# Gate and up of batches 2 and 3 by seven products of quarters in place of eight

## The chip, the cores and the metric

The kernel runs on one core of one Trainium2 chip. The metric is the device time of one execution in microseconds (us). Engines: TensorE (PE; its weight loads are PEld), VectorE (DVE), ScalarE (ACT), GpSimd (POOL) and SyncE (SP), which issues DMAs.

## The reference

One decoder layer, float32, 4 batches of 512 tokens of width 512:

```
x = layernorm(x + attention(x; Wqkv, bqkv, Wo, bo))        # 16 heads of 32
x = layernorm(x + wkv(w, u, k=x, v=ctx))                   # recurrence along the tokens
g = x @ Wg.T;  u = x @ Wu.T                                # 512 -> 2048, Wg = (gate_w - 128) * gate_scale
x = layernorm(x + (silu(g) * u) @ Wd.T)                    # 2048 -> 512
```

## The kernel before

Every engine's instruction stream is written out from one list of pieces, `tt.order`, that `timetable()` makes: tables of slot numbers at the head of the file (QK_AT, WKV_AT, YT_AT, X2_AT and others) say at which slot a piece is added, and each engine's block walks the list and issues what is its own. So each engine does its pieces strictly in the list's order, and waits on semaphores for the others.

Slots 0 to 255 are the attention of the 16 groups of heads (scores, exponentials, transposes, products with V), with the projections of later batches between them. From slot 256 on, four batches follow in turn: 16 tiles `it` of 128 gate and up features (`gu`, `gate_up`, L838), then four products with the down weights (`y`, L860 and L862; the last of all is cut in quarters, `y_quarters`, L849 and L851). Between them stand the recurrence of later batches (`wkv`: `ek` on ACT, `scan_q` and `scan_p` with the two scans L1181 and L1189, and four reciprocals L1195 in `divide`), and the transposes `yt` and `x2t`.

A token value is held as a high and a low half in float16 (x2h, x2l), transposed, so that each weight tile is multiplied with both. One tile `it` of one batch is, for gate and again for up, 4 tiles of the inner dimension by 2 halves: 16 matmuls of 128x128 weights by 512 tokens. Each half tile of a product fills one of the 8 PSUM banks, and `unit` gives a product the bank that is emptied first. For gate ACT takes silu out of PSUM (`th`, L1014); DVE multiplies by the up product in PSUM (`hf`, L1222); ACT makes the high half of the result (`hh`, L1024) and POOL the low one (`hl`, L1433). Nothing on PE waits for these but the down products and the reuse of banks.

Of the kernel before, what the change touches and what calls it, by code (L numbers as in the profile page):

```python
# [19 lines left out]
EPS = 1e-5  # L20
EOFF = {0: 0, 1: 128, 2: 384, 3: 768}
# [23 lines left out]

EARLY = 4


W_SPLIT = (6, 7, 8, 11)
V0_AT = (0, 8)  # L50
QK_AT = {2: (8, 17), 3: (10, 27), 4: (38, 48), 5: (57, 63), 6: (67, 75), 7: (79, 85), 8: (105, 112), 9: (124, 131),
         10: (136, 144), 11: (146, 151), 12: (166, 175), 13: (173, 195), 14: (195, 199), 15: (212, 228)}
V_AT = {1: (50, 57, 59, 82), 2: (117, 125, 132, 140), 3: (181, 195, 199, 205)}
WO_AT = {0: (86, 96, 100, 103), 1: (152, 154, 155, 168), 2: (203, 212, 216, 224)}
EARLY_AT = (246, 256)

FIN_AT = {0: (3, 0, 10), 1: (3, 2, 13), 2: (2, 0, 11), 3: (2, 0, 12), 4: (2, 1, 4), 5: (1, 0, 3), 6: (3, 1, 10),
          7: (4, 2, 10), 8: (3, 0, 14), 9: (4, 2, 5), 10: (1, 0, 7), 11: (4, 1, 7), 12: (3, 3, 6), 13: (3, 12, 15),
          14: (4, 2, 13)}

LAST_AT = (5, 5, 6)
WAIT = {'high': 1, 'low': 1, 'vtake': 1, 'r1': 2, 'norm': 4, 'exp': 4, 'eb': 0, 't1': 0, 't3': 0, 'oh': 2, 'ol': 2,
        'ek': 1, 'scan_q': 3, 'scan_p': 6, 'divide': 8, 'r2': 2, 'x2h': 1, 'x2l': 3, 'expand': 0}
WAIT_IN = {'r1': 6, 'norm': 2, 'ek': 1, 'scan_q': 1, 'scan_p': 1, 'divide': 2, 'r2': 0, 'x2h': 2, 'x2l': 2}
PIECE_AT = {'load_second': 41, 'small': 101, 'split_wo': 46, 'load_ds': 229}
WU_AT = (41, 71, 77, 116)
WU_ZERO = (83, 88, 137, 144)
WG_AT = (207, 207, 214, 215)
WG_ZERO = (224, 235, 241, 244)
# [8 lines left out]
YT_AT = {0: (156, 164, 174, 183), 1: (269, 270, 270, 270), 2: (283, 283, 286, 287), 3: (302, 303, 303, 308)}  # L78
X2_AT = {0: (225, 228, 230, 232), 1: (272, 272, 272, 273), 2: (290, 291, 291, 292), 3: (314, 314, 314, 314)}
WO_IN = (10, 11, 11, 14)  # L80
ZERO_IN = (8, 9, 11, 12, 12, 12, 12, 14, 14, 14, 14, 14, 14, 14, 14, 14)

KEYS = (0, 0, 0, 0)

TURN = ((4, 6, 5), (3, 4, 6), (3, 6, 5), (3, 4, 4))

OH_POOL = (1, 1, 0, 1, 0, 1, 1, 1, 0, 0, 0, 1, 0, 1, 1, 0)
XH_POOL = (0, 1, 1, 1)

COPIES = (5, 2, 0, 4, 1, 1, 0, 0, 0, 0, 0, 2, 2, 0, 0, 1)  # L90
# [53 lines left out]
def on_dve(H, item):  # L144
# [15 lines left out]
    "x2t": lambda b, c: ("x2l", b, c),  # L160
# [9 lines left out]
def timetable():  # L170
# [376 lines left out]
def build(nc, ctx, xT, x, ctxT, wqkv, bqk, bv, wo, bo, wcol, ucol, gateT, gsc, upT, usc, downT, dsc,  # L547
# [130 lines left out]

    def split_from(p):
# [15 lines left out]
    def stacked(n, kind, r):  # L695
# [3 lines left out]
                SCR[n, "qk".index(kind)][part].rearrange("(h p) t -> p h t", p=32))  # L699

# [3 lines left out]
    def _(e):  # L704
# [137 lines left out]

        def y_cut(q):
# [27 lines left out]
        for name, *a in tt.order:  # L871
# [41 lines left out]
    def _(e):  # L913
# [90 lines left out]

        def th(b, it):
# [600 lines left out]
```

## Time and profile before

| | us |
|---|---|
| median of 3 runs | 727.84 |
| lowest, highest | 725.76, 728.02 |
| profiled execution | 728.07 |
| its span, first to last instruction | 726.0 |
| PE busy | 707.3 |
| DVE, ACT, POOL busy | 510.8, 409.0, 303.2 |

The span is what the trace shows; 2.1 us lie around it. Matmuls overlap in the trace: one of 512 columns is listed with 0.38 us though the next starts 0.216 us later. So PE's busy time says when it has work, and not how fast it goes: that is read from the distance between starts.

### The profile page before, as it was taken

The page shows a single profiled execution, that of the slowest core. Times are in us where ns is not written, and L with a number is a line of the kernel's source. Part 1 is how long each engine was busy: PE and PEld are TensorE (multiplying, and loading weights), DVE is VectorE, ACT ScalarE, POOL GpSimd, SP SyncE. Part 2 cuts the span into 40 slices and gives each one's busy share as a digit, 9 for nine tenths or more (in the row PEclk, how much of TensorE's full clock was granted, in tenths as well). Part 3 has the DMA queues.
Part 4 walks back from the last instruction along what each step waited for, and adds up shares of the span by engine and source line. Part 5 has one row for each costly group of instructions (what it writes and reads, how often), then busy time and mean ns, then how long its engine had stood idle before and what let it go on. Part 6 is the DMA issues. An engine that isn't in the chain of part 4 may idle for free.

```text
span 726.0 us, 11976 instructions
## 1 busy us (share of the span) xinstructions
PE 707.3 (97%) x4274; PEld 391.4 (54%) x4274; DVE 510.8 (70%) x1191; ACT 409.0 (56%) x980; POOL 303.2 (42%) x338
## 2 busy tenths in 40 slices
PE   8898999999999999998999999999999999999997
PEld 3466665666665666666554445445544444544445
DVE  3588766799899889899826889866787734532224
ACT  5478877769886787679755662154612532133310
POOL 2016421464766314541356834474645733023310
PEclk9999999999999999999999999999999999999999
DMA  7728739344233234643044010000001000100001
GB/s 230 227 87 212 241 73 242 86 123 117 66 92 115 51 104 130 143 76 88 3 63 112 1 59 15 30 16 1 0 16 44 0 1 1 43 16 1 0 15 44
DMA packets 45530, 54.16 MB, mean 75 GB/s; under 512 B 4896, under 2 KB 34848, under 8 KB 45472
## 3 DMA queue, kind: packets, MB, share of 16 engines
q1 hardware_dynamic: 41632, 46.59, 21.9%
q0 software_dynamic: 3264, 6.29, 5.1%
q10 hardware_dynamic: 576, 0.52, 0.3%
q8 instruction: 34, 0.56, 0.3%
q14 instruction: 24, 0.20, 0.1%
HBM read 47.10 MB, written 12.58 MB: 82 GB/s over the span
## 4 chain that ended last, share of the span: by engine, by line
PE 87%; DVE 4%; ACT 3%; DMA 2%; issue 2%; SPq 1%; POOL 1%; ACTq 0%; POOLq 0%; DVEq 0%
PE psb L838 29%; PE psb L726 10%; PE psb L764 8%; PE psb L862 7%; PE psb L860 7%; PE psb L742 6%; PE psb L809 5%; PE psb L777 5%; PE psb L753 4%; PE psb L825 2%; PE psb L797 2%; PE psb L788 2%; DMA ks<-parts 1%; ACT ee L949 1%; DVE st L1143 1%
## 5 line engine op out<-in xcount | busy, mean ns | idle before, releaser
L1098 DVE CUSTOM_DVE_ANT_0 ee<-psb,mask,clip 128x512 f32<-128x512 f32 (+3 forms) x256 | 130.6, 535 | 20.7 <-PE psb L753 20.1
L949 ACT ACTIVATE ee<-ee,nm 128x512 f32<-128x512 f32 (+3 forms) x256 | 142.0, 559 | 1.5 <-DVE nm L1098 1.5
L1433 POOL TENSOR_TENSOR hl<-hf,hh 128x512 f16<-128x512 f32 x64 | 74.2, 1160 | 103.6 <-ACT hh L1024 103.6
L1024 ACT ACTIVATE hh<-hf 128x512 bf16<-128x512 f32 x64 | 40.3, 630 | 119.6 <-DVE hf L1222 115.1
L960 ACT ACTIVATE ee<-psb 128x256 f32<-128x256 f32 (+1 forms) x156 | 81.5, 531 | 42.7 <-PE psb L764 36.3
L764 PE MATMUL psb<-ident,ee 128*128 128x128 f32 x640 | 98.9, 274 | 3.3 <-DVE ee L1112 1.5
L1222 DVE SCALAR_TENSOR_TENSOR hf<-th,c,psb 128x512 f32<-128x512 f32 x60 | 43.7, 729 | 79.8 <-PE psb L838 63.2
L838 PE MATMUL psb<-x2h,wg 128*128 128x512 f16 x256 | 97.0, 379 | 0.0
L838 PE MATMUL psb<-x2h,wu 128*128 128x512 f16 x256 | 97.0, 379 | 0.0
L838 PE MATMUL psb<-x2l,wg 128*128 128x512 f16 x256 | 97.0, 379 | 0.0
L838 PE MATMUL psb<-x2l,wu 128*128 128x512 f16 x256 | 97.0, 379 | 0.0
L860 PE MATMUL psb<-wd,hh 128*128 128x512 f16 x240 | 91.0, 379 | 0.0
L862 PE MATMUL psb<-wd,hl 128*128 128x512 f16 x240 | 91.0, 379 | 0.0
L764 PEld LDWEIGHTS psb<-ident,ee 128*128 128x128 f32 x640 | 75.2, 141 | 24.1 <-ACT ee L960 3.0
L753 PE MATMUL psb<-ks,qs 128*128 128x512 f16 (+3 forms) x256 | 73.9, 300 | 4.0 <-DMA ks<-parts 2.5
L726 PE MATMUL psb<-xh,wqk 128*128 128x512 f16 x256 | 65.9, 384 | 2.1 <-ACT xh L921 1.1
L1195 DVE RECIPROCAL ek<-ek 128x128 f32<-128x128 f32 x64 | 58.0, 930 | 5.4 <-POOL ek L1401 5.4
L1385 POOL TENSOR_TENSOR rs<-ve,half 128x1 f32<-128x1 f32 (+1 forms) x24 | 17.3, 719 | 97.1 <-DVE ve L1163 96.9
L1014 ACT ACTIVATE th<-psb,g 128x512 f32<-128x512 f32 x60 | 40.8, 680 | 28.9 <-PE psb L838 28.7
L949 ACT ACTIVATION_READ_ACCUMULATOR ee<-ee,nm 128x1 f32 x256 | 50.7, 198 | 0.0
L838 PEld LDWEIGHTS psb<-x2l,wu 128*128 128x128 f16 x256 | 25.1, 98 | 29.9
L838 PEld LDWEIGHTS psb<-x2h,wu 128*128 128x128 f16 x256 | 25.1, 98 | 29.9
(130 smaller groups left out, 1215.7 us busy)
## 6 DMA issues: line engine op xcount, KB each, us to landing
qs<-parts SPq DMA_DIRECT2D x64, 128.0 KB, 2.9
ks<-parts SPq DMA_DIRECT2D x60, 128.0 KB, 3.4
parts<-qhl SPq DMA_DIRECT2D x16, 256.0 KB, 2.1
parts<-khl SPq DMA_DIRECT2D x16, 256.0 KB, 2.3
x<-in_x SPq DMA_DIRECT2D x4, 1024.0 KB, 6.9
ct<-in_ctxT SPq DMA_DIRECT2D x4, 1024.0 KB, 5.3
out<-x SPq DMA_DIRECT2D x16, 256.0 KB, 2.0
xt<-in_xT SPq DMA_DIRECT2D x14, 256.0 KB, 4.2
```

The costliest lines, as they stand in the source:

```text
L726: mm = e.matmul(PSB[:, bk, :], wt[:, k, c0:c0 + P], xt[:, k, :], start=(p == 0 and k == 0), stop=(p == 2 and k == T - 1))
L753: e.matmul(PSB[:, bank["score", H, i], 0:w], QS[:, sl, h, i * P:(i + 1) * P], KS[:, sl, h, 0:w], start=True, stop=True).then_inc(sem("scor ...
L764: mm = e.transpose(PSB[:, bk, o:o + P], E[H % 3][:, EOFF[i] + j * P:EOFF[i] + (j + 1) * P], IDENT[:])
L838: mm = e.matmul(PSB[:, bk, :], wt[:, k, it * P:(it + 1) * P], xt[:, s, k, :], start=(k == 0 and xt is x2h), stop=(k == T - 1 and xt is x2l))
L860: e.matmul(PSB[:, bk, :], HS[it][0][:, t * P:(t + 1) * P], wd[:, it, :], start=(it == 0), stop=False)
L862: mm = e.matmul(PSB[:, bk, :], HS[it][1][:, t * P:(t + 1) * P], wd[:, it, :], start=False, stop=(it == IT - 1))
L949: e.activation(dst, dst, ACT.Exp, bias=NM[:, n % 4, col:col + 1], scale=-1.0, accum_out=DEN[:, n % 4, col:col + 1]).then_inc(sem("exp"), 1)
L960: e.activation(ET[h][:, base:base + width], PSB[:, bank["turn", H, item], 0:width], ACT.Copy).then_inc(sem("et"), 1)
L1098: e.tensor_tensor_reduce(E[H % 3][:, EOFF[i]:EOFF[i] + w], PSB[:, bank["score", H, i], 0:w], MASK[:, S - w:S], -SC, CLIP[:, i:i + 1], ALU. ...
L1195: e.reciprocal(EK2S[c % 2][:, cut], EK2S[c % 2][:, cut]).then_inc(sem("rcp"), 1)
L1222: e.scalar_tensor_tensor(out=half[:], in0=gated[:], scalar=col, in1=PSB[:, bank["up", b, it], :], op0=ALU.mult, op1=ALU.mult).then_inc(sem ...
L1433: e.tensor_tensor(HS[it][1][:], ring(b, it)[1][:], HS[it][0][:], ALU.subtract).then_inc(sem("hl"), 1)
```

## The change

For batches 2 and 3 (`SEVEN`), gate and up are taken together as one product of a 2 by 2 block matrix of weights (gate and up by the two halves of the inner dimension) with a 2 by 2 block matrix of tokens (the same halves by tokens 0 to 255 and 256 to 511), and its four quarters are made from seven products of quarters, not eight. Three of the seven need sums of weight quarters only, made once (`weight_sum`: 8 of 128x2048 float16 values, 4 on DVE, 4 on POOL), three need sums of token quarters (`x_sum`, then high and low halves again), and results are added up in and behind PSUM. A pair `m` is two tiles `it`: seven `product` calls of 8 matmuls of 256 columns. Products 1, 6, 7 and 4 run on in one bank ("sa"), 5 and 3 in another ("sd"), 2 in a third ("sb"). Between them ACT copies the bank's value so far to SBUF (`snap1`, `snap5`, `snap6`) and the next product of the bank waits for that; DVE adds the copies (`c11`, `c12`, `c22`). silu now reads SBUF, two per pair behind `c12`, and the multiplication is cut in halves of 256 tokens (`hfb`, `hfa`). Product 4 of a pair comes in the next pair.

The core of the diff:

```diff
+SEVEN = (2, 3)
-WKV_AT = {(0, 0): 111, (0, 1): 123, (0, 2): 133, (0, 3): 143, (1, 0): 191, (1, 1): 209, (1, 2): 262, (1, 3): 264,
-          (2, 0): 266, (2, 1): 272, (2, 2): 274, (2, 3): 277, (3, 0): 288, (3, 1): 292, (3, 2): 294, (3, 3): 297}
+WKV_AT = {(0, 0): 111, (0, 1): 123, (0, 2): 134, (0, 3): 144, (1, 0): 193, (1, 1): 208, (1, 2): 263, (1, 3): 266,
+          (2, 0): 268, (2, 1): 271, (2, 2): 273, (2, 3): 277, (3, 0): 285, (3, 1): 289, (3, 2): 291, (3, 3): 296}
-REST_AT = (16, 41, 97, 72)
+REST_AT = (0, 36, 92, 13)
...
+    def seven_first(b, m):
+        if m == 0:
+            tt.flush(("xlo", b, 3))
+        for j, name in ((1, "sa"), (5, "sd"), (2, "sb"), (6, None)):
+            if name:
+                tt.unit(name, b, m)
+                tt.unfinished.add((name, b, m))
+            add("p", b, m, j)
+            if j == 2:
+                add("c11", b, m)
+            else:
+                add(f"snap{j}", b, m)
+
+    def seven_second(b, m):
+        for j in (3, 4, 7) if m < PAIRS - 1 else (4, 7, 3):
+            if j == 4:
+                fourth(b, m - 1)
+                continue
+            add("p", b, m, j)
...
+                add("c12", b, m)
+            else:
+                add("c22", b, m)
+        for it in (2 * m, 2 * m + 1):
+            add("silu", b, it)
+        for it in (2 * m - 2, 2 * m - 1) if m else ():
+            add("hh", b, it)
+            add("hl", b, it)
+        for it in (2 * m, 2 * m + 1):
+            add("hfb", b, it)
...
+        def product(b, m, j):
...
+            if j == 6:
+                pe.wait_ge(*by("snap1", b, m))
+            elif j == 7:
+                pe.wait_ge(*by("snap6", b, m))
+            elif j == 4:
+                pe.wait_ge(*by("c22", b, m))
+            elif j == 3:
+                pe.wait_ge(*by("snap5", b, m))
+            for k in (0, 1):
+                for kk in (0, 1):
+                    for low in (0, 1):
+                        mm = e.matmul(PSB[:, bk, k * HALF_S:(k + 1) * HALF_S], weights(j, kk, 2 * m + k),
+                                      moving(b, j, kk, low), start=(unit is not None and k + kk + low == 0),
+                                      stop=(kk + low == 2), skip_group_check=True)
...
+        def silu(b, it):
+            m, k = divmod(it, 2)
+            act.wait_ge(*by("c11", b, m))
+            act.wait_ge(*by("c12", b, m))
+            e.activation(pair(b, m)[:, k, :], pair(b, m)[:, k, :], ACT.Silu, scale=G2[:, it:it + 1]).then_inc(sem("silu"), 1)
```

Nearly all other tables of slots are changed as well (QK_AT, V_AT, TURN and the rest, REST_AT as an example above), so that pieces of the attention stand in another order; COPIES gives DVE 24 of the copies of transposed scores in place of 36, and KEYS gives POOL one multiplication per column tile of batch 0.

Where the last column tile of the recurrence (batch 3) falls in batch 2, DVE's queue held this before (names: hf, the multiplication; ekv, qs_, ps, the recurrence and its scans; ek2, its reciprocals):

```order
L1222 SCALAR_TENSOR_TENSOR hf1<-th1,c2,psb 128x512
L1222 SCALAR_TENSOR_TENSOR hf2<-th2,c2,psb 128x512
L1177 TENSOR_TENSOR ekv<-ek,ct 128x512
L1181 SCALAR_TENSOR_TENSOR qs_<-ew,ek 128x512
L1189 SCALAR_TENSOR_TENSOR ps<-ew,ekv 128x512
L1222 SCALAR_TENSOR_TENSOR hf0<-th0,c2,psb 128x512
L1195 RECIPROCAL ek2_1<-ek2_1 128x128 x2
L1222 SCALAR_TENSOR_TENSOR hf1<-th1,c2,psb 128x512
```

It holds this now (ring01 with 2x256 first `c11`, then `c12`; ct2<-psb `c22`; 128x256 `hfb` or `hfa`):

```order
L1517 TENSOR_TENSOR ring01<-psb,snap1 128x2x256
L1449 TENSOR_TENSOR ekv<-ek,ct 128x512
L1453 SCALAR_TENSOR_TENSOR qs_<-ew,ek 128x512
L1461 SCALAR_TENSOR_TENSOR ps<-ew,ekv 128x512
L1523 TENSOR_TENSOR ring01<-psb,ys 128x2x256
L1529 TENSOR_TENSOR ct2<-psb,ct2 128x512
L877 SCALAR_TENSOR_TENSOR ring01<-ring01,c2,ct2 128x256 x2
L1467 RECIPROCAL ek2_1<-ek2_1 128x128 x2
L1517 TENSOR_TENSOR ring01<-psb,snap1 128x2x256
L1467 RECIPROCAL ek2_1<-ek2_1 128x128 x2
L1523 TENSOR_TENSOR ring01<-psb,ys 128x2x256
L877 SCALAR_TENSOR_TENSOR ring01<-ring01,c2,psb 128x256 x2
```

The recurrence stood behind two multiplications; now it stands between `c11` and `c12` of the first pair, and its reciprocals are on both sides of `c11` of the second.

ACT's queue at the same place before (ek: the two exponentials of the recurrence; th: silu):

```order
L988 ACT_TABLE_LOAD
L988 ACTIVATE ek<-psb,nmu 128x512
L991 ACTIVATE ek2_1<-psb,mu2 128x512
L1014 ACT_TABLE_LOAD
L1014 ACTIVATE th0<-psb,g2 128x512
L1024 ACTIVATE hh2<-hf0 128x512
L1014 ACTIVATE th1<-psb,g2 128x512
L1024 ACTIVATE hh3<-hf1 128x512
```

And now, from the second copy of batch 2's first pair (snap1, ct2 and ys written from psb are the copies, ring01 by g2 silu):

```order
L1253 ACTIVATE ct2<-psb 128x512
L1253 ACTIVATE ys<-psb 128x512
L1196 ACTIVATE ek<-psb,nmu 128x512
L1199 ACTIVATE ek2_1<-psb,mu2 128x512
L1259 ACT_TABLE_LOAD
L1259 ACTIVATE ring01<-ring01,g2 128x512 x2
L1253 ACTIVATE snap1<-psb 128x512
L1253 ACTIVATE ys<-psb 128x512 x2
L1259 ACTIVATE ring01<-ring01,g2 128x512 x2
L1265 ACTIVATE hh0<-ring01 128x512
L1265 ACTIVATE hh1<-ring01 128x512
L1253 ACTIVATE snap1<-psb 128x512
```

The copies of a pair now stand behind silu and `hh` of the pair before, in one queue, and the table load in front of the first silu carries its wait for `c12`.

## Rows read from the trace of the kernel before

**Rows 1.** The page, part 1: busy us (share of the span) xinstructions.
```profile
PE 707.3 (97%) x4274; PEld 391.4 (54%) x4274; DVE 510.8 (70%) x1191; ACT 409.0 (56%) x980; POOL 303.2 (42%) x338
```

**Rows 2.** Windows: us, busy PE, PEld, DVE, ACT, POOL (xinstructions), PEclk, DMA share, GB/s.
```profile
20.00:380.00 360.00, 350.87 (x2482) 218.51 (x2481) 295.75 (x860) 274.33 (x784) 147.95 (x197) 1.00 0.45 116
...
460.00:550.00 90.00, 90.00 (x442) 43.96 (x441) 67.25 (x97) 34.56 (x50) 50.36 (x44) 1.00 0.04 16
550.00:693.00 143.00, 142.99 (x681) 66.94 (x679) 60.96 (x95) 46.63 (x71) 51.54 (x46) 1.00 0.03 10
```

**Rows 3.** The chain that ended last, in order of time: start us, us, what.
```profile
637.50 55.25 PE psb L838 x256
```

**Rows 4.** PE's timeline, the last 128 matmuls (first and last): start us, us, engine.
```profile
713.31 0.22 PE L849 MATMUL psb<-wd,hh 128*128 128x128 f16 x1
...
720.40 0.22 PE L851 MATMUL psb<-wd,hl 128*128 128x128 f16 x1
```

**Rows 5.** PEld's timeline beside them (one of the 128 weight loads).
```profile
713.59 0.10 PEld L849 LDWEIGHTS psb<-wd,hh 128*128 128x128 bf16 x1
```

**Rows 6.** Groups of one shape, ACT: busy us, mean ns, idle before.
```profile
L960 ACT ACTIVATE ee<-psb 128x512 f32<-128x512 f32 x108 | 63.2, 597 | 23.7 <-PE psb L764 23.3
...
L1014 ACT ACTIVATE th<-psb,g 128x512 f32<-128x512 f32 x60 | 40.8, 680 | 28.9 <-PE psb L838 28.7
L1024 ACT ACTIVATE hh<-hf 128x512 bf16<-128x512 f32 x64 | 40.3, 630 | 119.6 <-DVE hf L1222 115.1 <-PE psb L788 4.6
...
L1014 ACT ACT_TABLE_LOAD x9 | 11.5, 1283 | 0.2
```

**Rows 7.** The same, DVE.
```profile
L1222 DVE SCALAR_TENSOR_TENSOR hf<-th,c,psb 128x512 f32<-128x512 f32 x60 | 43.7, 729 | 79.8 <-PE psb L838 63.2 <-ACT th L1014 13.5 <-issue 2.9
...
L1233 DVE TENSOR_TENSOR ys<-psb,bo 128x512 f32<-128x512 f32 x15 | 10.1, 671 | 31.4 <-PE psb L862 31.4
...
L1200 DVE TENSOR_SCALAR wu<-wu 128x2048 f16<-128x2048 f16 x4 | 3.6, 893 | 0.0
...
L1079 DVE SCALAR_TENSOR_TENSOR wv<-ee,wv 128x2048 f16<-128x2048 f32 x1 | 2.3, 2291 | 1.0 <-ACT wv L926 1.0
...
L1253 DVE TENSOR_TENSOR x<-ys,x 128x128 f32<-128x128 f32 x4 | 1.2, 292 | 0.1
```

**Rows 8.** The same, POOL.
```profile
L1433 POOL TENSOR_TENSOR hl<-hf,hh 128x512 f16<-128x512 f32 x64 | 74.2, 1160 | 103.6 <-ACT hh L1024 103.6
L1397 POOL TENSOR_TENSOR ct<-ek,ct 128x512 f32<-128x512 f32 x16 | 32.2, 2011 | 8.8 <-DVE ekv L1177 8.1
```

**Rows 9.** ACT's timeline where its queue is full.
```profile
440.81 0.69 ACT L988 ACTIVATE ek<-psb,nmu 128x512 f32<-128x512 f32 x1 [3.37 <-PE psb L825]
441.40 0.68 ACT L991 ACTIVATE ek<-psb,mu 128x512 f32<-128x512 f32 x1
```

**Rows 10.** DVE's timeline, one column tile of the second stage.
```profile
547.82 0.68 DVE L1177 TENSOR_TENSOR ekv<-ek,ct 128x512 f32<-128x512 f32 x1
...
549.55 2.22 DVE L1189 TENSOR_TENSOR_SCAN ps<-ew,ekv 128x512 f32<-128x512 f32 x1
552.86 2.58 DVE L1195 RECIPROCAL ek<-ek 128x128 f32<-128x128 f32 x3 [1.09 <-POOL ek L1401]
```

**Rows 11.** All engines, where ACT starts behind a gate product.
```profile
663.23 0.38 PE L838 MATMUL psb<-x2h,wu 128*128 128x512 f16 x1
...
663.43 0.69 ACT L1014 ACTIVATE th<-psb,g 128x512 f32<-128x512 f32 x1 [0.26 <-PE psb L838]
```

**Rows 12.** Windows around PE's idle time at 22 us (columns as in rows 2).
```profile
22.00:25.00 3.00, 1.24 (x6) 0.32 (x4) 1.79 (x6) 1.09 (x2) 0.00 (x0) 1.00 0.58 186
25.00:28.80 3.80, 3.73 (x10) 1.38 (x11) 1.35 (x7) 1.80 (x8) 0.00 (x0) 0.55 0.78 208
```

**Rows 13.** PE's timeline there, eight 512-column matmuls.
```profile
25.34 3.52 PE L742 MATMUL psb<-wv,xh 128*128 128x512 f16 x8
```

**Rows 14.** Who PE waited for: us in total, times, longest us.
```profile
PE psb L753 <- DMA ks<-parts: 2.5, 2, 1.5
```

More of the change, by code:

```diff
@@ L20 @@
 EPS = 1e-5
+HALF_S = S // 2
 EOFF = {0: 0, 1: 128, 2: 384, 3: 768}
@@ L44 @@
 OHS = 6
+SEVEN = (2, 3)
+PAIRS = IT // 2
+SIGNAL = {"snap1": "snap", "snap5": "snap", "snap6": "snap", "c11": "summed", "c12": "summed", "c22": "summed"}
+PART_READ = {1: 1, 2: 0, 3: 0, 4: 3, 5: 1, 6: 2, 7: 2}
 EARLY = 4
[L49 to L53, printed above, removed]
@@ L62 @@
[L62 to L69, printed above, removed]
@@ L79 @@
[L79 to L90, printed above, removed]
+LAST_AT = (5, 5, 8)
+WAIT = {'high': 1, 'low': 1, 'vtake': 1, 'r1': 2, 'norm': 6, 'exp': 4, 'eb': 0, 't1': 1, 't3': 0, 'oh': 2, 'ol': 3,
+        'ek': 1, 'scan_q': 2, 'scan_p': 7, 'divide': 8, 'r2': 3, 'x2h': 1, 'x2l': 2, 'expand': 0}
@@ L159 @@
     "yt": lambda b, t: ("r2", b, t),
-    "x2t": lambda b, c: ("x2l", b, c),
+    "x2t": lambda b, c: ("xf" if b in SEVEN else "x2l", b, c),
+    "sa": lambda b, m: ("hfa", b, 2 * m + 1),
+    "sb": lambda b, m: ("c11", b, m),
+    "sd": lambda b, m: ("c12", b, m),
     "gate": lambda b, it: ("aa" if early(b, it) else "th", b, it),
@@ L295, in x2t, with quarters @@
         add("x2t", b, c)
+        if b in SEVEN:
+            late(wait("x2h"), lambda: quarters(b, c))
+            return
         late(wait("x2h"), lambda: add("x2h", b, c))
         late(wait("x2l"), lambda: add("x2l", b, c))
+    def quarters(b, c):
+        add("xf", b, c)
+        if c == T - 1:
+            for k in range(4):
+                add("xhi", b, 0) if k == 0 else None
+                add("xt", b, k)
+                add("xhi", b, k) if k else None
+            for k in range(4):
+                add("xlo", b, k)
     def gu_parts(b, it, pools):
@@ L433, in timetable @@
         piece(max(BO_AT[b], PIECE_AT["split_wo"] + 2), "add_bo", b)
+    for j, slots in WS_AT.items():
+        for kk, slot in enumerate(slots):
+            piece(slot, "ws", j, kk)
     for which, slot in WKV_AT.items():
@@ L1066, in _ @@
                 th(*a)
+            elif name == "xf":
+                x_full(*a)
+            elif name == "xhi":
+                x_part_high(*a)
+            elif name in ("snap1", "snap5", "snap6"):
+                snap(*a, int(name[-1]))
+            elif name == "silu":
+                silu(*a)
+            elif name == "hh" and a[0] in SEVEN:
+                hh_seven(*a)
             elif name == "hh":
@@ L1322, in _ @@
                 hf(*a)
+            elif name == "ws" and not WS_POOL[a[0] - 1]:
+                weight_sum(e, dve, *a)
+            elif name == "xt":
+                x_sum(*a)
+            elif name == "xlo" and not XLO_POOL[a[0]]:
+                x_part_low(e, dve, *a)
+            elif name == "c11":
+                c11(*a)
+            elif name == "c12":
+                c12(*a)
+            elif name == "c22":
+                c22(*a)
+            elif name == "hfa":
+                hf_half(e, dve, *a, True)
+            elif name == "hfb" and not HFB_POOL[a[0]]:
+                hf_half(e, dve, *a, False)
             elif name == "yd":
@@ L1474, in _ @@
                 hl(*a)
+            elif name == "ws" and WS_POOL[a[0] - 1]:
+                weight_sum(e, pool, *a)
+            elif name == "xlo" and XLO_POOL[a[0]]:
+                x_part_low(e, pool, *a)
+            elif name == "hfb" and HFB_POOL[a[0]]:
+                hf_half(e, pool, *a, False)
     @block.sync
```

245 lines of the change are left out of this document (223 added, 22 removed).

## The prediction

> **What bounds the kernel now.** I read the page's busy shares first, then busy time by stage, the chain that ended last, who PE waited for, and at the end single shapes and timelines. PE is busy 707.3 of 726.0 us, DVE 510.8 and the others less [rows 1]. By stage the reader should see that PE is busy 142.99 of the 143 us from 550 to 693, which are batches 2 and 3 almost whole, and all 90 us before them, while DVE, ACT and POOL are there busy 61, 47 and 52 of 143 us [rows 2]. The chain says the same: gate and up of batch 3 are one unbroken piece of 256 matmuls in 55.25 us [rows 3], 215.8 ns each. So in the stage that is changed every 100 ns taken from PE is 100 ns of the span, as long as nothing new makes PE wait. In the attention, 20 to 380 us, PE is without work 9.1 us and DVE is busy 296 of 360 [rows 2].
>
> **What the change takes from PE.** Before, a pair of tiles is 32 matmuls of 512 columns (2 tiles, gate and up, 4 inner tiles, 2 halves): 32 x 0.2158 = 6.91 us. Now it is 7 products of 8 matmuls of 256 columns. No row shows 256 columns in a dense stream, but both sides do: 128 columns start 55.8 ns apart (720.40 - 713.31 over 127 steps [rows 4]), 512 columns 215.8 ns. The line through the two gives 109.1 ns, of which some 2.4 ns don't depend on columns. A pair is then 56 x 0.1091 = 6.11 us, 0.80 less, and for 16 pairs the term is **-12.7 us**. The bounds are 107 ns (half of 512 columns, 14.6 us gained) and 112 ns (twice the 128, 10.1 gained). I take the line, since both its ends are the same kind of float16 stream.
>
> The change doubles the weight loads per column, and a load is listed with 0.10 us [rows 5]. Each of those 128-column matmuls has its own load and they still start 55.8 ns apart, so loads overlap and do not set a distance of 109 ns. The Trainium skill speaks against this: TensorE: Matmul & The Clock Gate, Back-to-back issue gap, says that in a stream of load and matmul pairs the load has its share in the spacing, and gives about 81 ns at 128 columns and 131 at 512. By a line through those (98 ns at 256) the sum would be 16 x (56 x 0.098 - 32 x 0.131) = +20 us, an estimate from that page. The trace has 55.8 and 215.8 at its two points, so I go by the trace.
>
> **What it adds on PE's path: waits.** PE never waited for an elementwise result in gate and up. Now each bank goes on only after ACT has copied it. In a steady pair, product 6 needs snap1, which stands in ACT's queue behind two silu and two `hh` of the pair before, which stand behind `c12`, which stands behind product 3. From product 6 round to the next product 6: two products 1.75 us, handover 0.20 (the gate product ends at 663.23 and ACT starts at 663.43 [rows 11]), `c12` 0.67 like the addition from PSUM [rows 7], then silu, silu, hh, hh, copy. Those take 0.68, 0.63 and 0.60 [rows 6], but in a full queue the next starts 0.09 before the one before it ends (441.40 after 440.81 with 0.69 [rows 9]): 0.59 + 0.59 + 0.54 + 0.54 + 0.60 = 2.86. With 0.1 for two handovers between the others the ring is 5.6 us, against 6.11 that PE needs: no wait, 0.5 to spare. DVE has three additions and four half multiplications (0.44 each, between 292 ns for 128 and 729 for 512 columns [rows 7]), 3.8 of 6.11 us; POOL two `hl` of 1.16 [rows 8].
>
> The exception is the last column tile of the recurrence, which now stands between `c11` and `c12` of the first pair of batch 2. Counting from product 1's start: product 6 ends at 3.49, the transposes at 3.93, ACT's first exponential at 4.82. DVE then has the multiplication and two scans, 3.95 us from 547.82 to 551.77 [rows 10], until 8.8, then `c12` until 9.5. The table load, 1.28 [rows 6], has the wait for `c12` on it: 10.8. Two silu 12.05, snap1 12.6. PE is ready for product 6 at 8.3 and **waits 4.3 us**. In the second pair two of the four reciprocals (0.86 each, three in 2.58 [rows 10]) stand before `c11` and two before `c12`: second `hfb` 12.5, `c11` 15.0, `c12` 17.45, silu, hh and copy 20.3, where PE is ready at 18.7: **1.6 us** more. A residual and a norm before `c11` of the last pair cost 0.3. Sum **+6.2 us**. Bounds: 4 (if DVE starts the scans earlier or the load goes ahead of its wait, 1.3 less) and 10 (no overlap in ACT's queue, where the ring is 5.9, and each handover a little longer).
>
> **What it adds elsewhere, at nothing.** Four weight sums on DVE, of 2048 float16 each, lie between 0.89 and 2.29 us [rows 7], at most 9.2; DVE is idle 22.7 of the 90 us from 460 to 550 [rows 2]. Four on POOL are 4.6 us each by `hl`, up to 8.0 by the slower form [rows 8]; POOL is idle 39.6 of these 90, and a late `hl` holds back only the third multiplication after it, with 8 banks behind that. If that cover were gone, each would cost PE its excess over some 8 us. The sums of tokens (4 copies of 0.60, 4 additions of 0.7, 4 high halves up to 1.1, low halves on POOL 8.1 together) make a chain that ends, by my count, 25.7 us after the down products start, and the products give it 28.1; at POOL's slower rate it would end 4 us late, in each of two batches. These are the bounds, 0 and 8; I take 0. The attention's new order: the 9.1 us of waiting there could shrink or grow. x of batch 0 and of batch 3 are now loaded early, beside the stacks of q and k, for which PE already waited 2.5 us [rows 14]. DVE gives 12 copies of 0.7 to ACT, which has 86 us free. I take 0, between -5 and +5.
>
> **The clock.** In 22 to 25 us PE was busy 1.24 of 3 us at full clock; in the 3.8 us after it the granted clock was 0.55 [rows 12], mostly the 1.2 GHz level, and eight matmuls of 512 columns took 3.36 us to the start of the next work in place of 1.73 [rows 13]. So a wait of 4.3 us may well be followed by such a stretch, which costs 1.6. Here it lands between the two waits, where DVE and not PE sets the end, so I count 0. The Trainium skill (the same page, HAM oscillation) has the rule that idle gaps between bursts put the clock back and the warming is paid again; by it the 1.6 would be paid once per gap, and it would be hidden as above.
>
> **Sum.** 728.07 (the profiled execution, 726.0 of span and 2.07 around it) - 12.7 + 6.2 = 721.6; the median of the runs is 0.2 lower than that execution, and I add 0.5 for handovers not counted: **722**.
>
> **Rivals.**
> 1. *The waits hardly come* (0.20). If the planner's order lets DVE do the scans under product work, or the early stages win a few us, 12.7 stays nearly whole with 1 to 2 of waits: **716**. Against it stand the queues: `c12` cannot pass the scans.
> 2. *The head of batch 2 costs more* (0.14): the token sums are late at POOL's slower rate, or the low clock is not hidden: +3, **725**.
> 3. *The attention loses what the products gain* (0.12): loads beside the stacks and new places cost PE 5 us more. The row for it is the wait for ks; against it, PE is busy 351 of 360 us there. **727.5**, no difference.
> 4. *The ring becomes the bound* (0.07), slower. If silu from SBUF, the strided additions or each handover cost more than their nearest rows, PE waits in all 14 steady pairs. The 6.5 us of gain are gone when the ring is 6.6 us, 1.0 above my count; at 7.1 us it is 14 x 1.0 = 14 more: **735**. Against it: everything in the ring has a row within 10%.
> 5. *Weight loads set the distance* (0.02), slower: with a load of 98 ns before each 56 ns of work it would be 0.154 x 56 = 8.6 us a pair, 27 us more than before: **755**. The 128-column stream speaks against it [rows 4]. It is the skill's rule above.
>
> That the change does not do what it says I rule out: the order of instructions shows 56 matmuls of 256 columns per pair.
>
> **How the numbers follow.** The forecast has 0.45. The range of 8 in 10 leaves out rivals 4 and 5 and the ends of 1: from 715 to 730. A measurement of this kernel can tell 0.3%, some 2.2 us, from no change. Faster: 0.45 + 0.20 + 0.14 = 0.79; the same: rival 3, 0.12; slower: rivals 4 and 5, 0.09.
>
> **What would show it.** In the changed profile: matmuls of 256 columns 109 ns apart; one pair 6.11 us from product 1 to product 1 in batch 3, with PE not waiting; two waits of PE, 4 and 1.6 us, for ACT's copy to snap1 at the head of batch 2, with DVE in the scan and the reciprocals then; the granted clock low behind the first; DVE busier in batches 2 and 3 by some 38 us (16 x 3.8 against 32 x 0.73) and ACT by 29 (16 x 4.42 against 32 x 1.31). It is wrong if PE waits for snap1 in every pair, if the distance is over 112 ns, or if the attention ends more than 5 us earlier or later than 380.

## The result, and the profile after

| | before | after |
|---|---|---|
| median of 4 runs, us | 727.31 | **744.62** |
| lowest, highest | 725.76, 728.02 | 743.99, 746.62 |
| profiled execution (span) | 728.07 (726.0) | 743.99 (742.0) |

The ratio is 1.0246, 95% interval 1.0219 to 1.0272: slower by 17 us, where 722 was forecast and 730 was the end of the range. The page, busy us of each engine:

```profile
PE 703.0 (95%) x4658; PEld 430.2 (58%) x4658; DVE 580.9 (78%) x1259; ACT 444.1 (60%) x1052; POOL 346.7 (47%) x350
```

Against [rows 1], PE has less to do and waits more; DVE is busy 70 us longer and POOL 43, in part because their instructions take longer and not only because there are more of them. The windows, columns as in [rows 2]:

```profile
20.00:380.00 360.00, 348.71 (x2448) 215.70 (x2450) 291.29 (x844) 278.40 (x799) 146.82 (x192) 0.99 0.42 113
...
460.00:550.00 90.00, 87.87 (x424) 42.47 (x422) 78.77 (x100) 36.78 (x52) 69.78 (x50) 0.98 0.03 9
550.00:693.00 143.00, 129.89 (x968) 96.49 (x967) 114.75 (x168) 63.12 (x105) 62.47 (x47) 0.95 0.04 16
```

PE was without work 0 us from 460 to 693 before; now it lacks 2.1 and then 13.1 us, and the granted clock, 1.00 before, is 0.98 and 0.95. DVE is busy 115 of 143 us where it was 61, 54 more and not the 38 of the prediction; POOL's busy time from 460 to 550 rose from 50 to 70 us. Who PE waited for (us in total, times, longest), those that are new or larger; the second and third fall in the attention:

```profile
PE psb L1044 <- ACT snap L1253: 10.1, 3, 8.2
PE psb L932 <- DVE nm L1370: 4.6, 8, 1.4
PE psb L998 <- DMA ct<-in_wo: 2.8, 1, 2.8
PE psb L1044 <- POOL x2l L864: 2.5, 1, 2.5
PE psb L1017 <- DVE x2l L1477: 2.1, 1, 2.1
PE psb L1066 <- DVE x L1422: 1.1, 1, 1.1
PE psb L1044 <- DVE ys L1529: 0.4, 1, 0.4
```

That the products themselves pay as forecast shows in the chain, where PE runs on without a wait (start, us, what), first in batch 2 behind its head, then in batch 3:

```profile
595.42 17.48 PE psb L1044 x160
...
667.64 41.31 PE psb L1044 x376
```

160 matmuls in 17.48 us are 109.3 ns each, 376 in 41.31 are 109.9. Batch 3 takes 49.5 us from its first product at 659.31 to the first down product at 708.79, against 55.25 before [rows 3]: 5.8 gained of 6.35. The loss lies ahead of it: batch 2 begins at 563.5 us, and began at 550.3 before; batch 3 begins at 659.3, and began at 637.3. So 13 us are lost before the first new product, and 9 more in batch 2.

**A norm that takes 4.2 us.** DVE's timeline and POOL's in y of batch 0 (start, us):

```profile
448.41 0.94 DVE L1467 RECIPROCAL ek<-ek 128x128 f32<-128x128 f32 x1
449.27 4.17 DVE L1441 TENSOR_SCALAR x<-x,mv,rs 128x512 f32<-128x512 f32 x1
453.36 0.94 DVE L1467 RECIPROCAL ek<-ek 128x128 f32<-128x128 f32 x1
```

```profile
449.10 4.05 POOL L859 TENSOR_TENSOR s1a<-wu 128x2048 f16<-128x2048 f16 x1
```

The norm of 512 columns has a median of 0.55 us. It takes 4.17 here, and ends 0.3 us after POOL's weight sum, which began just before it, has ended. The same stands at 547.80 (4.16, beside the sum from 547.62 to 551.68). The steps behind it in DVE's queue are late too, for DVE has no gap in its work from there to 471 us: PE waits 1.14 us at 454.90 for a residual and 2.13 at 471.02 for the low half that opens batch 1, and the first matmuls behind that wait are at the low level of the clock (32 of them take 8.6 us, from the start of the first to that of the next work, in place of 6.91).

**The head of batch 2.** All engines, from the token sums to the wait (a few lines of each, in order of time):

```profile
558.51 4.86 POOL L864 TENSOR_TENSOR x2l<-ring,x2h 128x1024 f16<-128x1024 f32 x2
561.43 2.49 DVE L1509 TENSOR_TENSOR snap<-ring 128x512 f32<-128x512 f32 x1
563.34 2.57 POOL L864 TENSOR_TENSOR ct<-ring,ct 128x1024 f16<-128x1024 f32 x1
563.52 0.27 PE L1044 MATMUL psb<-x2h,wg 128*128 128x256 f16 x1 [2.54 <-POOL x2l L864]
563.85 2.34 DVE L1441 TENSOR_SCALAR x<-x,mv,rs 128x512 f32<-128x512 f32 x1
...
573.68 0.68 DVE L1517 TENSOR_TENSOR ring<-psb,snap 128x512 f32<-128x512 f32 x1
574.88 1.22 DVE L1453 TENSOR_TENSOR_SCAN qs_<-ew,ek 128x512 f32<-128x512 f32 x1
576.01 2.22 DVE L1461 TENSOR_TENSOR_SCAN ps<-ew,ekv 128x512 f32<-128x512 f32 x1
578.15 0.66 DVE L1523 TENSOR_TENSOR ring<-psb,ys 128x512 f32<-128x512 f32 x1
578.89 1.28 ACT L1259 ACT_TABLE_LOAD   x1 [8.03 <-DVE ring L1523]
582.06 0.61 PE L1044 MATMUL psb<-ct,s2a 128*128 128x256 f16 x2 [8.18 <-ACT snap L1253]
```

The fourth token sum takes 2.49 us and the norm behind it 2.34, both beside POOL's low halves, and PE waits 2.54 us for those. DVE then works off the last two residuals and norms of batch 1, with two gaps of 0.66 us, and comes to the first `c11` only at 573.68, though PE was through with product 2 at 567.8. From there it goes as the prediction has it: scans, `c12`, table load, copy. PE waits 8.18 us. Behind it 27 matmuls start 0.214 us apart, half the speed, until 587.84: 2.8 us more than at 0.109. Behind the wait of 2.54 it was the same for 3.2 us, 1.6 more.

### The profile page after: what moved, and what is told of

Its sections match the earlier page's. It is cut to its first block, busy times and chain, and to the rows that moved or that the text cites. A ratio compares the mean times of both kernels' runs of the same rounds, so it can differ in the third digit from the quotient of the medians.

```text
span 742.0 us, 13026 instructions
## 1 busy us (share of the span) xinstructions
PE 703.0 (95%) x4658; PEld 430.2 (58%) x4658; DVE 580.9 (78%) x1259; ACT 444.1 (60%) x1052; POOL 346.7 (47%) x350
## 4 chain that ended last, share of the span: by engine, by line
PE 60%; DVE 19%; issue 7%; ACT 5%; DMA 4%; POOL 3%; SPq 1%; ACTq 0%; POOLq 0%; DVEq 0%
PE psb L1044 10%; PE psb L1017 9%; PE psb L905 8%; PE psb L943 7%; PE psb L921 5%; PE psb L988 4%; PE psb L956 4%; DVE x L1441 4%; PE psb L932 4%; PE psb L1068 2%; PE psb L1066 2%; DMA ct<-in_wo 2%; DVE ek L1467 2%; DVE st L1415 2%; DVE ps L1461 2%
## 5 line engine op out<-in xcount | busy, mean ns | idle before, releaser
L1755 POOL TENSOR_TENSOR hl<-ring,hh 128x512 f16<-128x512 f32 x64 | 80.5, 1272 | 94.6 <-ACT hh L1265 55.9
L1168 ACT ACTIVATE ee<-psb 128x512 f32<-128x512 f32 (+1 forms) x168 | 84.4, 526 | 35.4 <-PE psb L943 33.0
L1017 PE MATMUL psb<-x2h,wg 128*128 128x512 f16 x128 | 49.1, 384 | 2.1 <-DVE x2l L1477 2.1
L1017 PE MATMUL psb<-x2l,wg 128*128 128x512 f16 x128 | 49.3, 385 | 0.0
L1017 PE MATMUL psb<-x2h,wu 128*128 128x512 f16 x128 | 48.9, 382 | 0.0
L1017 PE MATMUL psb<-x2l,wu 128*128 128x512 f16 x128 | 48.8, 381 | 0.0
L1441 DVE TENSOR_SCALAR x<-x,mv,rs 128x512 f32<-128x512 f32 x48 | 40.9, 897 | 7.1 <-POOL rs L1707 7.1
L932 PEld LDWEIGHTS psb<-ks,qs 128*128 128x128 f16 x256 | 24.9, 98 | 30.2 <-DVE nm L1370 8.1
L1066 PEld LDWEIGHTS psb<-wd,hh 128*128 128x128 bf16 x240 | 23.5, 98 | 29.0 <-DVE x L1422 1.4
L1068 PEld LDWEIGHTS psb<-wd,hl 128*128 128x128 f16 x240 | 23.5, 98 | 28.5 <-POOL hl L1755 0.9
```

Source lines behind the costliest of these rows:

```text
L932: e.matmul(PSB[:, bank["score", H, i], 0:w], QS[:, sl, h, i * P:(i + 1) * P], KS[:, sl, h, 0:w], start=True, stop=True).then_inc(sem("scor ...
L1017: mm = e.matmul(PSB[:, bk, :], wt[:, k, it * P:(it + 1) * P], xt[:, s, k, :], start=(k == 0 and xt is x2h), stop=(k == T - 1 and xt is x2l))
L1066: e.matmul(PSB[:, bk, :], HS[it][0][:, t * P:(t + 1) * P], wd[:, it, :], start=(it == 0), stop=False)
L1068: mm = e.matmul(PSB[:, bk, :], HS[it][1][:, t * P:(t + 1) * P], wd[:, it, :], start=False, stop=(it == IT - 1))
L1168: e.activation(ET[h][:, base:base + width], PSB[:, bank["turn", H, item], 0:width], ACT.Copy).then_inc(sem("et"), 1)
L1755: e.tensor_tensor(HS[it][1][:], pair(b, it // 2)[:, it % 2, :] if b in SEVEN else ring(b, it)[1], HS[it][0][:], ALU.subtract).then_inc(sem ...
```

## The experiments

Each run was made beside runs of the kernel before on the same chip: e1 to e4 on one (before: 728.2 us), e5 to e8 on a second (726.9), e9 to e12 on a third (726.8). Times are medians; ratios to before with their 95% interval. A difference between two groups is safe to about 1 us: by the ratios e2 less e11 is 3.9 us, by the medians 4.8.

| run | us | ratio |
|---|---|---|
| the change | 744.6 | 1.0246 (1.0219 to 1.0272) |
| e1, weight sums on DVE | 736.1 | 1.0115 (1.0080 to 1.0149) |
| e2, all sums on DVE | 734.4 | 1.0093 (1.0062 to 1.0125) |
| e3, eight products, new order | 735.2 | 1.0119 (1.0082 to 1.0156) |
| e4, scans later | 747.6 | 1.0279 (1.0249 to 1.0310) |
| e5, seven products, old order, sums on DVE | 740.4 | 1.0167 (1.0134 to 1.0199) |
| e6, old order, seven in batch 3 alone | 726.4 | 0.9981 (0.9959 to 1.0004) |
| e7, new order, seven in batch 3 alone | 730.5 | 1.0045 (1.0023 to 1.0066) |
| e8, POOL's weight sums cut in four | 736.9 | 1.0133 (1.0108 to 1.0157) |
| e9, e6 with the sums later | **723.0** | 0.9937 (0.9913 to 0.9960) |
| e10, e2 with the attention's old order | 729.1 | 1.0028 (1.0011 to 1.0044) |
| e11, e2 with the old places of the loads of x | 729.6 | 1.0040 (1.0022 to 1.0059) |
| e12, e2 with short scans | 730.7 | 1.0047 (1.0028 to 1.0067) |

### Do POOL's long instructions hold DVE? (e1, e2, e8)

```diff
-WS_POOL = (1, 0, 0, 1)
+WS_POOL = (0, 0, 0, 0)
```

> All eight weight sums on DVE, none on POOL. Theory L (one long POOL instruction holds up DVE's instructions on SBUF until it ends): DVE's norm steps at 449 and 548 us, 4.17 and 4.16 us in the changed kernel, fall to their usual 0.55, and PE's waits before batch 1's gate (1.1 and 2.1 us) with the slow clock behind them (1.8) go; DVE takes on four sums of 1.2 to 2.2 us. Time 738 to 741, from 744.6. Theory Q (DVE is late because of what stands in its own queue, and the long norm records are only how it waits): the four more sums, some 7 us of DVE work, make it later still, 745 to 749.

e2 has besides:

```diff
-XLO_POOL = (0, 0, 1, 1)
+XLO_POOL = (0, 0, 0, 0)
```

> The weight sums and also the low halves of the token sums on DVE, so POOL does no new work at all. Theory L: the second and third token sums, 2.5 us each beside POOL's low halves, fall to 0.7; the low halves, 2.5 to 4.9 us on POOL, take about 1.1 for 1024 elements on DVE; PE's wait of 2.5 us for them before batch 2 goes, and the first addition c11 of batch 2 comes some 4 us earlier, so the wait for snap1 falls from 8.2 towards the 4.3 that the scans alone cost: 733 to 737. Theory Q: the same DVE queue gets 4 us more per batch: the head waits grow, 746 to 752.

And e8 keeps the sums on POOL:

```diff
-        e.tensor_tensor(WSUM[j][kk], a, c, op).then_inc(sem(f"ws{j}"), 1)
+        for w in range(4 if WS_POOL[j - 1] else 1):
+            cut = slice(w * 512, (w + 1) * 512) if WS_POOL[j - 1] else slice(0, I)
+            ins = e.tensor_tensor(WSUM[j][kk][:, cut], a[:, cut], c[:, cut], op)
+        ins.then_inc(sem(f"ws{j}"), 1)
```

> The changed kernel with each of POOL's four weight sums cut into four instructions of 512 columns; same work, same queue places. Theory L (the two engines hold the way to SBUF for a whole instruction): DVE's norm at 449 and 548 us is held 1.0 to 1.5 us in place of 4.2, and the time is near e1's, 736 to 740. Theory R (they share it, each slowed in proportion): DVE's instructions there are as slow in sum as before, and the time stays 743 to 746.

e1 took 8.5 us off, more than its expectation, and e2 10.2, though both give DVE more to do; so theory Q falls. These two also free POOL's queue, so they don't show by themselves that it is DVE that was held. e8 is the clean test, for it moves no work at all: 7.7 us off. DVE and then POOL in e8 at the place shown above:

```profile
447.78 1.27 DVE L1444 TENSOR_SCALAR x<-x,mv,rs 128x512 f32<-128x512 f32 x1
```

```profile
447.61 4.67 POOL L861 TENSOR_TENSOR s1a<-wu 128x512 f16<-128x512 f16 x4
```

The four pieces take 4.67 us together, against 4.05 for the sum in one, and the norm is held 1.27 us, about one piece. That speaks for a hold by the instruction (L) and against a shared rate (R). In e1 the norm at 452.07 took 0.45. The wait of 2.54 us at the head of batch 2 is gone in e8 as well, though the low halves of the token sums are still on POOL there: it was the weight sum at 547.62, holding the norm, that made them late. The wait for snap1 stays 8.17 us in e8 and 8.2 in e1, so these holds are not its cause. What is left of the waits in e2:

```profile
PE psb L1044 <- ACT snap L1253: 8.0, 2, 7.5
PE psb L1017 <- DVE x2l L1477: 0.9, 1, 0.9
```

The waits before batches 1 and 2 are down to 0.9 and nothing, the token sums to 0.69 each. The wait for snap1, which I expected to fall towards 4.3, fell only to 7.48. That part of the expectation was wrong.

### What makes the wait of 7.5 to 8.2 us? (e4, e12)

```diff
-          (2, 0): 268, (2, 1): 271, (2, 2): 273, (2, 3): 277, (3, 0): 285, (3, 1): 289, (3, 2): 291, (3, 3): 296}
-YT_AT = {... 3: (300, 301, 307, 308)}
+          (2, 0): 268, (2, 1): 271, (2, 2): 273, (2, 3): 277, (3, 0): 285, (3, 1): 289, (3, 2): 291, (3, 3): 299}
+YT_AT = {... 3: (303, 303, 307, 308)}
```

> The last column tile of the recurrence (x1t, exponentials, scans) stands behind the second pair of batch 2 and its reciprocals round the third, in place of between c11 and c12 of the first; its transposes yt of the first two token tiles follow 2 to 3 tiles later. Theory S (the scans behind a late c11 make the wait): the first wait for snap1 falls from 8.2 us to under 3, a wait of 2 to 4 appears behind the second pair instead, where DVE has caught up; in all 3 to 5 us less: 739 to 742. Theory L (DVE is behind by the locked 7 us whatever the order, so the same wait comes at another place): 743 to 746.

747.6, against 744.6 for the change: above both ranges. It is not better; that it is worse isn't shown, since the two intervals overlap. The larger of PE's seven waits for snap1 in e4:

```profile
567.72 0.38 PE L1044 MATMUL psb<-ct,s2a 128*128 128x256 f16 x2 [1.74 <-ACT snap L1253]
577.88 0.39 PE L1044 MATMUL psb<-ct,s2a 128*128 128x256 f16 x2 [4.70 <-ACT snap L1253]
587.50 0.39 PE L1044 MATMUL psb<-ct,s2a 128*128 128x256 f16 x2 [1.24 <-ACT snap L1253]
598.25 0.39 PE L1044 MATMUL psb<-ct,s2a 128*128 128x256 f16 x2 [4.46 <-ACT snap L1253]
```

One wait of 8.2 has become four of 1.2 to 4.7 in the first pairs, and PE's total for snap1 rose from 10.1 to 15.2. Theory S falls: the scans' place alone is not the cause.

```diff
+            w = 8 if (b, c) == (3, 3) else S
-            e.tensor_tensor_scan(QS_[:, 1:S + 1], EW[:, c:c + 1].broadcast_to([P, S]), EK[:], 0.0, ALU.mult,
+            e.tensor_tensor_scan(QS_[:, 1:w + 1], EW[:, c:c + 1].broadcast_to([P, w]), EK[:, 0:w], 0.0, ALU.mult,
...
-            cut = slice(k * P, (k + 1) * P)
+            cut = slice(k * P, k * P + (8 if (b, c) == (3, 3) else P))
```

> e2, where the two scans and four reciprocals of the last column tile of the recurrence do only their first 8 columns (of 512 and of 128), so that the last quarter of v's features is left out. DVE has 3.2 us less between c11 and c12 and 3.0 less round the second pair. Prediction's account of the wait (4.3 us from the scans alone): the wait for snap1 falls from 7.5 to about 4 and the second one stays gone, since c11 itself comes 4 us late out of the y phase: 730 to 732. Rival (ACT's queue, its exponentials and the table load set the wait, not DVE): it stays above 6, 733 to 735.

```profile
PE psb L1044 <- ACT snap L1253: 4.9, 2, 4.4
```

The longest wait went from 7.48 to 4.4 and the time down by 3.6 us. So the scans make 3.1 us of it, and 4.4 us are there without them. About 1 of the 3.1 is again a hold: in e2 the second scan takes 2.23 us beside POOL's product of 2.04 (568.82), and in e12, with the short scans, the same product takes 1.26 (567.02). The 4.4 fit DVE's backlog out of the y phase: in e2, PE is through with the first product 2 at 562.5 and DVE begins the first `c11` at 567.4. No run takes this backlog away, so that part is read from the trace and not tested. ACT's table load (1.28 us) and two silu stand behind `c12` in both runs and are part of what is left; that they set the wait instead of DVE is refuted by the fall of 3.1. In e2 DVE has that backlog without any hold by POOL's sums (columns of windows as in [rows 2]):

```profile
538.00:576.00 38.00, 30.52 (x182) 17.71 (x181) 34.35 (x49) 12.37 (x19) 16.41 (x14) 0.95 0.08 28
```

34.35 of 38 us busy: DVE is close to the bound of this stretch. The corresponding 38 us before (530 to 568) have 31.28, with PE never waiting, since nothing on PE hung on DVE then.

### What does the new order cost? (e3, e10, e11, e5)

```diff
-SEVEN = (2, 3)
+SEVEN = ()
...
-    for j, slots in WS_AT.items():
-        for kk, slot in enumerate(slots):
-            piece(slot, "ws", j, kk)
```

> Eight products in batches 2 and 3 as before and no weight or token sums, but all the changed tables (order of the attention, places of the recurrence). It prices the new order alone. If the order costs what the trace suggests (the attention ends 3.9 us later, and y of batch 0 some 2 more without the sums' part): 731 to 734. If what looked like the order's cost was pressure of the sums on DVE and POOL: 727 to 729. Batches 2 and 3 take 6.91 us per pair again and PE never waits there.

735.2, above the upper branch: the tables alone cost 7 us (6 to 11 by the interval), without one new product or sum. In batches 2 and 3 PE waits for nothing, as expected. The trace has 3.5 us of the loss before the first gate product (355.7 us against 352.2) and 2.6 between there and batch 2. The tables hold more than places: they also give ACT 12 of DVE's copies.

```diff
-REST_AT = (0, 36, 92, 13)
+REST_AT = (16, 41, 97, 72)
```

> e2 with x of batches 0 and 3 loaded at the slots of before (16 and 72 in place of 0 and 13). If these loads delay the load of Wo (PE waited 2.7 us for it) and the stacks: 731 to 733, from 734.4. If Wo's load is late for another reason (its wait for the staged tokens): 734 to 735.

729.6, 4.8 us less than e2 and more than I expected. But I had named the wrong batches; the edit puts back all four. In the changed kernel the last large load ahead of Wo's in SP's queue is that of batch 1, moved from slot 41, where it stood behind Wo's, to 36:

```profile
64.64 0.43 SPq L1853 DMA_DIRECT2D x<-in_x  x1
68.39 0.61 SPq L1859 DMA_DIRECT2D ct<-in_wo  x1
```

In e11 Wo's load is issued at 69.27 us and this one at 76.03. The changed kernel's chain and the timeline of PE behind it; then the same product in the kernel before:

```profile
68.39 14.45 DMA ct<-in_wo
82.97 5.12 PE L998 MATMUL psb<-ct,bv 128*128 128x512 f32 x8 [2.77 <-DMA ct<-in_wo]
```

```profile
80.09 3.60 PE L819 MATMUL psb<-ct,bv 128*128 128x512 f32 x8
```

Wo takes 14.45 us to land, 9.9 before; PE waits 2.77 us, and the eight matmuls behind take 5.12 in place of 3.60, since the clock has fallen (0.84 from 83 to 92 us). In e11 Wo lands after 10.0 us, the wait is gone and they take 3.60 again. That it is this one of the four loads is read from the queue; no run moves it alone.

e10 takes every table of the attention from before (and with it the recurrence's places and others up to slot 255, and the shares of DVE, ACT and POOL), those behind it from the change, and has all sums on DVE.

> Tables of the attention (slots to 255) as before the change, those from slot 256 on as after it; seven products in batches 2 and 3, all sums on DVE. The new order's 7 us from e3 split in two: if they are lost in the attention (the trace shows 3.9 us by its end, PE waiting 4.6 us for the masked scores on DVE and 1.7 to 3 for the load of Wo), this runs at 734.4 - 4 = 729 to 731. If they are lost behind slot 256: 733 to 736.

729.1, only 0.5 us below e11: nearly all that the attention loses lies in the places of these loads. The many short waits for the scores' maxima (nm), 4.6 us in e11 and 2.4 in e10, are worth no more than that. The rest of the 7 us lies behind slot 256.

e5 goes on and takes those as before too (WKV_AT, YT_AT, X2_AT, WAIT_IN, WO_IN, ZERO_IN and LAST_AT).

> Every table of slots as it was before the change; seven products in batches 2 and 3; all weight and token sums on DVE. If the new order costs the 7 us that run e3 showed whatever stands behind it: 734.4 - 7 = 727 to 729. If the new order was what made room for the sums on DVE between 460 and 575 us (there the recurrence's fifteenth column tile stands in the y phase again), the head of batch 2 waits 4 to 6 us longer: 731 to 734.

740.4: wrong in both branches, and the slowest of the runs with all sums on DVE. PE's waits for snap1:

```profile
PE psb L1044 <- ACT snap L1253: 17.6, 4, 15.3
```

With the old places the fifteenth column tile of the recurrence falls into y of batch 1, and one wait, at the head of batch 2, is 15.3 us. DVE begins the first `c11` at 569.39, and in front of the copy ACT now also has a second table load and the exponentials of the last column tile (573.40 to 575.85). So behind slot 256 the new order loses some 2 us by itself and saves 11 for seven products (e5 less e10). The two can't be judged apart.

### Seven products where DVE has room (e6, e7, e9)

```diff
-SEVEN = (2, 3)
+SEVEN = (3,)
...
-WS_AT = {1: (272, 280), 2: (280, 283), 3: (277, 281), 4: (282, 292)}
+WS_AT = {1: (298, 299), 2: (300, 301), 3: (303, 304), 4: (305, 306)}
```

and all sums on DVE; e6 with all tables of before, e7 with those of the change.

> Tables of before, seven products in batch 3 alone, weight sums on DVE spread over batch 2, where DVE was busy 61 of 143 us, token sums on DVE. No recurrence is left by then. Theory D (DVE's saturation from 538 to 573 us, the stretch with recurrence, y's steps and sums, is what eats the gain): batch 3 keeps its gain of 6.35 less a wait of 1 to 3 at its head: 722 to 725 against 728 before. Rival (any head of a batch with seven products costs its wait of 8 us, because of the token sums and the ring's filling): 728 to 731.

> The same with the changed tables. Against e3 (735.2, the same tables with eight products) it prices seven products in batch 3 alone: 729 to 732 by theory D, 735 to 738 by its rival. With e6 it gives the price of the new order a second time, 7 us if it is independent of the products.

e6: 726.4, between the two expectations and not distinguishable from before. e7: 730.5, 4.7 us below e3, as theory D has it. e7 less e6 is 4.1 us and not 7: the new order's price depends on what stands behind it. The head of batch 3 costs 0.66 us of waits in e6, not 8. But PE waited elsewhere:

```profile
PE psb L1004 <- POOL ct L1735: 2.5, 1, 2.5
```

```profile
573.63 2.00 DVE L859 TENSOR_TENSOR s2a<-s1a,wg 128x2048 f16<-128x2048 f16 x1
```

```profile
571.09 2.21 POOL L1755 TENSOR_TENSOR hl<-ring,hh 128x512 f16<-128x512 f32 x1 [1.15 <-ACT hh L1286]
574.51 2.14 POOL L1755 TENSOR_TENSOR hl<-ring,hh 128x512 f16<-128x512 f32 x1
```

Here DVE holds POOL: a low half `hl` takes 2.1 to 2.2 us beside the weight sums in place of 1.16, and the recurrence's last product stands behind it. e9 moves the sums behind the recurrence:

```diff
-WS_AT = {1: (298, 299), 2: (300, 301), 3: (303, 304), 4: (305, 306)}
+WS_AT = {1: (304, 305), 2: (306, 307), 3: (305, 308), 4: (309, 310)}
```

> e6 with the weight sums moved behind the last column tile of the recurrence (from the ninth to the fifteenth tile of batch 2 in place of the third to the eleventh). In e6, PE waited 2.5 us for the recurrence's last product on POOL, whose low halves beside the sums took 2.1 us in place of 1.16. Theory L: this wait goes, 723 to 725 against 727 before, which would beat both kernels. Rival (the sums press on whatever stands there, now the norm and the transposes before batch 3): the wait comes back before batch 3, 726 to 728.

723.0 us, the interval wholly below 1: this version beats both kernels, the one before by 3.9 us or 0.6%. The wait for POOL is gone: batch 2 takes PE 57.6 us up to its down products, as before, and took 60.1 in e6. That e9 as a whole is faster than e6 is less sure: the profiled executions are 722.4 and 722.3 us (for e6 the fastest of ten), and the intervals just touch.

## Why the prediction was wrong

**"What the change takes from PE", 12.7 us: right.** The distance of 256-column matmuls was forecast as 109.1 ns and is 109.3 to 109.9, and weight loads don't set it. A pair takes 6.1 us in steady state, and PE waits for snap1 in none of the steady pairs (once for 0.31 us, in the second pair of batch 3). The rivals of the ring and of the weight loads didn't come. One bound was wrongly worked out: half of 512 columns is 107.9 ns, which gains 13.8 us, and not 107 and 14.6.

**"What it adds elsewhere, at nothing": this step failed.** I covered the sums by the idle time of DVE and of POOL, each by itself, with a bound of 8 us. Giving the sums to DVE alone takes 10.2 us off (e2); 7.7 already go with cut instructions and no work moved (e8). The mechanism was in rows that I had read and used as prices. The second scan takes 1.22 us in its shortest case of 16 in the kernel before; the 2.22 of [rows 10] is one held by POOL's product beside it; and the 2011 ns of POOL's product against 1160 for the same size [rows 8] is the other side of it, for its own shortest case of 16 takes 1.27. I called that "POOL's slower rate" and asked only how long POOL would take, not whom it would stop. The chain of token sums, which I let end 2.4 us before PE needs it, ended 2.5 late; without the hold of the norm ahead of it (e8) PE doesn't wait for it.

**The wait at the head of batch 2: the mechanism was right, the term mis-sized.** Forecast 4.3, measured 8.18. The scans are 3.1 us of it (e12). The count started with an empty DVE queue at product 1; the residuals and norms of batch 1 stood there, behind the token sums. The wait of 1.6 for the reciprocals didn't come, since PE itself was slow there, by 2.8 us. That of 0.3 near the last pair was 1.65: two residuals with their statistics stood before `c12`, where I had counted one residual and a norm before `c11`, and ahead of them two `hfb` took 2.56 us, from 614.95, beside an `hl` that began at 614.78. In e2 the `hl` begins behind them, they take 1.78, and the wait is 0.53.

**"The attention's new order", 0 between -5 and +5: it cost 4 to 5 us, at the edge of its bounds.** e2 less e10 is 5.3 us (4.7 by the ratios). In the eight traces with the new tables PE begins the first gate product at 356.0 us on average, in the five with those of before at 351.4: 4.6 us. I feared the loads beside the stacks of k, but PE's wait for those fell from 2.5 to 1.1 us; I didn't read what now stands ahead of Wo's load, and putting the loads back gives 4.8 us (e11). The rest of e3's 7 us lies between the first gate product and batch 2, for which the sum had no term.

**The clock, 0: wrong.** I expected its stretch to be hidden between two waits. It came behind each of the four waits over 2 us: 1.5 us on Wo's eight matmuls, 1.7 at the head of batch 1, 1.6 and 2.8 at that of batch 2. Only the last was hidden in part, as it took the place of the forecast wait of 1.6; the others ran out in dense work.

**Load of DVE, 54 us more from 550 to 693 us instead of 38.** The instructions of the pairs are 34 of it. `hfb`, which was priced at 0.44 us from its width, reads SBUF alone and runs beside `hl`: 0.71 and 0.89 on average, by the tile that it reads. The token sums, 12.8 us, were not in the 38, and the norms are 9.8 us more.

From forecast to result: 722.0, POOL's sums 10.2 (e2), the attention's new order 5.3 (e2 less e10), and 7.1 left, makes 744.6. The last is what remains, not a measurement of its own. Where it lies shows in the times at which PE begins the gate products of each batch, in one execution of each kernel (differences from before; the first stretch alone scatters by up to 4 us between runs that share its tables):

| stretch | before, us | forecast | the change | e2 | e3 | e10 |
|---|---|---|---|---|---|---|
| start to the gate of batch 0 | 352.2 | 0 | +4.0 | +5.7 | +3.5 | -1.7 |
| from there to batch 2 | 198.2 | 0 | +9.2 | +3.8 | +2.6 | +3.8 |
| batch 2 with its down products | 87.0 | -0.2 | +8.8 | +4.0 | +0.1 | +5.0 |
| batch 3 to the end | 88.7 | -6.4 | -6.0 | -6.2 | +0.1 | -6.2 |

With POOL's sums and the attention's order taken out (e10), some 4 us are lost before batch 2, most of them with the tables behind slot 256 and without any sum (e3), and 5 at the head of batch 2, where the wait is larger than forecast and the clock is low behind it.

The rival that came nearest was the second, "the head of batch 2 costs more". It had one of the places, the token sums and the clock, but with +3 us not the size. The third, at +5 us for the attention, had that part nearly right, though by another load. Nothing named a hold of one engine by the other.

## What to carry to other kernels

Idle time of two engines isn't cover for work on both of them: before giving POOL a long elementwise instruction, look in the trace for a DVE instruction beside one of POOL's, both on SBUF, that takes longer than its shortest of the same shape, and cut POOL's into short ones where it can't be moved. Where a change makes TensorE depend on an engine for the first time, count that engine's backlog from where it last was idle, and not from the start of the new stage. And of a reordered program the transfers are read too: what stands ahead of each large load in its queue.

## What was not expected of the hardware

- Some DVE instructions on SBUF stand still until a POOL instruction on SBUF that began before them has ended: the norm took 4.17 us for 0.55, and 1.27 where POOL's was cut in four; the additions and multiplications of two tensors from SBUF, and the scans, were held too. In all four cases in which a single norm of the changed kernel began beside a long one of POOL's, it ended 0.3 us after POOL's. Instructions of DVE that read one tensor from PSUM were not held (0.68 us at 566.12 beside POOL's from 565.87), nor were the statistics of the norm (0.69 to 0.70 in all 47 cases, at least 8 of them wholly within one of POOL's) and the reciprocals (0.89 to 0.95 each). It goes the other way too: `hl` 2.2 us in place of 1.16, and the recurrence's product 2.04 beside the scans (e2) and 1.26 beside short ones (e12). The Trainium skill says this (SBUF — State Buffer, Who interferes with whom): GpSimd's one port pair is DVE's second, and whoever starts first has it alone for its whole instruction. The trace agrees, for the norm, which has one tensor from SBUF, as well as for the sums, which have two. I hadn't weighed this rule in the prediction.
- The granted clock fell behind waits of 2.1, 2.5, 2.8 and 8.2 us. The stretch at the lower of the two levels (1.2 GHz) was 3.0 us long behind the first (512-column matmuls 0.43 us apart from 471.72 to 474.71), 3.2 behind the second and 5.8 behind the last. Behind the wait of 0.85 us in e2 at the same place as the first it stayed at 1.00 (470 to 482 us), and behind that of 1.65 in the changed kernel too (625 to 632).
